# Linear attention and a two-expert layer on one core: channel-major operand stacks made by DMA transposes instead of TensorE transposes and ScalarE copies

## Chip, core and metric

The kernel runs on one core of one Trainium2 chip. The metric is the device time of one execution in microseconds (us), median of several runs; lower is better. Engines are named as in the profile: PE (TensorE matmul), PEld (its weight load), DVE (VectorE), ACT (ScalarE), POOL (GpSimd), SP (SyncE, which here only issues DMAs).

## What is computed

The input x has 8 frames of 32 channels by 64 x 64 positions (4096 tokens). Cut to what matters:

```python
def conv(x):                      # on x normalised over its channels
    q, k, v = split(einsum('bcxy,oc->boxy', x, w_qkv) + b_qkv)     # 4 heads of 32
    q = softmax(q, over the 32 channels of a head) * scale
    k = softmax(k, over the 4096 tokens)
    context = einsum('bhdn,bhen->bhde', k, v / n)
    out = einsum('bhde,bhdn->bhen', context, q)
    return layernorm_over_channels(einsum('bcxy,oc->boxy', out, w_out) + b_out) * g_ln

x = x + conv(layernorm_over_channels(x))
t = tokens(x)                     # (8, 4096, 32)
n = layernorm(t)
probs = softmax(n @ router_w + router_b)          # 8 experts
top_p, top_i = top_k(probs, 2); top_p = top_p / sum(top_p)
t = t + sum of top_p * (n @ expert_w[top_i] + expert_b[top_i])
```

## The kernel before, in words

A frame lies in SBUF token-major: 128 partitions (tokens) by 32 tiles of 32 channels, 1024 numbers a partition. Matmuls that contract over the channels need the data channel-major. For that, each of two normalised tensors (`xhat`, called k=1, which feeds keys and queries; `xhat3`, k=3, which feeds router and experts) is split into float16 parts: ACT writes the high part twice (`high_parts`, L495 and L496), DVE writes the low part (`low_part`, L684), and the rest of the 128 columns are ones. The result, `parts[k]`, is 128 x 32 x 128 float16, 1 MB. Each of its 32 tiles of 128 x 128 is transposed into `stack[k]`, 128 x 4096 float16. In the kernel before, PE does it in four units of eight transposes each into the PSUM tile `narrow` (`make_stack`, L904 to L911, recorded on L842, the line of the helper `tr`), and ACT copies each unit to SBUF (`copy_stack`, L488 to L491).

The frames run through a software pipeline written out by hand. In iteration i of the program, every engine works on up to four frames: `nxt` (frame i+1: keys, maxima, context), `cur` (frame i: queries, attention, second normalisation), `prev` (frame i-1: router, experts, output) and `ahead` (frame i+2: load and first normalisation). An iteration has 26 steps, and tables such as `AT_QEXP` or `AT_KMAX` say at which step each unit of work stands; within a step the order is that of the code, and each engine executes its own list in order. Iterations 1 to 5 are a hardware loop (`Fori`, L302); the others are written out.

The names that matter here:
- PE: `query_logits` (eight units, steps 0 to 5; matmul `narrow<-stack,w_stack` of 512 columns and four of `narrow<-qmax_tr,maxpick`); ACT exponentiates each unit into `eq` (`query_exp`, L510) and by that frees its half of `narrow`; `attend` (eight units, steps 1 to 7, `wide<-mixz,eq`); DVE normalises each into `heads` (L703, L705).
- `router` (step 4): 32 small matmuls of all of `stack[3]`; ACT copies the logits (L536), DVE picks the two experts in 14 small steps (`route`, L754 to L777, steps 4 to 8).
- `key_logits_by_channel` (steps 7 to 10, `wide<-stack,w_stack` of 512 columns), one unit for each quarter of `stack[1]`; DVE takes the maximum of each (`kmax`, L713). The key maximum is needed before the keys' exponentials and everything behind them.
- `make_stack(3)` stands at steps 1, 1, 2, 3 and `make_stack(1)` at steps 6, 6, 7, 8.
- SP issues one load of x (512 KB) and one store of y (512 KB) in an iteration, load first, and waits for the end of each store before it goes on:

```python
def store(b):
    sp.wait_ge(y_ready, OUTU * b + OUTU)
    sp.dma_start(out_v[...], y_out[:, :]).then_inc(stored, 16)
    sp.wait_ge(stored, 16 * b + 16)
    sp.sem_inc(y_free, 1)
```

Of the kernel before, what the change touches and what calls it, by code (L numbers as in the profile page):

```python
# [44 lines left out]
XT, STACK, KEXP = 2, 4, 8  # L45
# [16 lines left out]
AT_SPLIT3 = 22  # L62

AT_STACK3 = (1, 1, 2, 3)
# [16 lines left out]
AT_STACK1 = (6, 6, 7, 8)  # L81
# [15 lines left out]
def build(nc, x, w_qkv, b_qkv, w_out, b_out, g_ln, router_w, router_b, expert_w, expert_b, out):  # L97
# [6 lines left out]
    with ctx:  # L104
# [125 lines left out]
        parts_ready = {k: sem(f"parts_ready{k}") for k in (1, 3)}  # L230
        kmax_nat_ready = sem("kmax_nat_ready")
# [10 lines left out]
        y_free = sem("y_free")  # L242
# [20 lines left out]
        class Places:  # L263
# [4 lines left out]
            def __init__(self, i, cur, prev, nxt, ahead):  # L268
                if isinstance(i, int):

                    a, b, c, d = (min(max(i + k, 0), NB) for k in (2, 1, 0, -1))
                    self.w, self.n, self.s = 8 * b + 8 * c + 8 * d, 2 * a + 14 * b + 8 * c + 4 * d, 3 * b + d
                else:
                    self.w, self.n, self.s = 24 * i, 28 * i + 14, 4 * i + 2
                w = n = s = 0
                self.qexp, self.norm, self.gate, self.kmax, self.qmax = {}, {}, {}, {}, {}
                self.xt, self.qrows, self.kexp, self.stack = {}, {}, {}, {1: {}, 3: {}}
# [4 lines left out]
                for step in STEPS:  # L282
                    for there, table, at in ((ahead, self.xt, AT_XT), (prev, self.stack[3], AT_STACK3),
                                             (cur, self.qexp, AT_QEXP), (nxt, self.stack[1], AT_STACK1),
# [10 lines left out]
        def run(engine, iteration, set_up=None):  # L295
# [6 lines left out]
            with engine.Fori(1, NB - 2) as i:  # L302
                iteration(i, True, True, True, True)
# [18 lines left out]
        def _(sp):  # L322
# [157 lines left out]
        def _(act):  # L480
# [32 lines left out]
            def copy_output(g, u):  # L513
                act.wait_ge(out_full, OUTU * g + u + 1)
                if u == 0:
                    act.wait_ge(y_free, g + 1)
                nc.scalar.copy(y_out[:, 512 * u:512 * u + 512], sums[:, :]).then_inc(y_ready, 1)

            def iteration(i, cur, prev, nxt, ahead):
                f, g, n, m, pos = i, i - 1, i + 1, i + 2, Places(i, cur, prev, nxt, ahead)  # L520
                for step in STEPS:
# [6 lines left out]
                    for u in units(prev, AT_STACK3, step):  # L528
                        copy_stack(3, pos, u)
# [18 lines left out]
                    for u in units(nxt, AT_STACK1, step):  # L548
                        copy_stack(1, pos, u)
# [287 lines left out]
        def _(pe):  # L837
# [30 lines left out]
            def query_logits_by_token(pos, u):  # L868
                pe.wait_ge(narrow_free, pos.n + pos.stack[1][u] + 1)
# [34 lines left out]
            def make_stack(k, pos, b, u):  # L904
                if u == 0:
                    pe.wait_ge(parts_ready[k], 2 * b + 2)
                wait_slot(pe, narrow_free, pos.n + pos.stack[k][u], 2)
                for t in range(8):
                    ins = tr(narrow[:, pos.stack[k][u] % 2, P // 2 * t:P // 2 * t + P // 2].bitcast(f16),
                             parts[k][:, 8 * u + t, :], ident16[:])  # L910
                ins.then_inc(narrow_full, 1)  # L911

            def key_logits_by_channel(pos, u):
                pe.wait_ge(narrow_free, pos.n + pos.stack[1][u] + 1)
# [37 lines left out]
            def router(pos):  # L952
# [88 lines left out]
```

## Time and profile before

| | |
|---|---|
| runs | 587.24 us median (587.27, 586.05, 587.24) |
| span of the profiled execution | 586.6 us, 10066 instructions |
| busy | PE 412.2 us (70%), PEld 327.8 (56%), DVE 411.6 (70%), ACT 236.5 (40%), POOL 219.2 (37%) |
| DMA queue of SP | 4216 packets, 8.59 MB, 5.0% of 16 engines |
| granted TensorE clock | 0.846 of full, mean |

The profiled execution's own time isn't listed apart from its span; the span is 0.64 us below the median of the runs. An iteration of the loop takes about 63.7 us (ACT starts the casts of `parts[3]` at 168.13, 232.22, 295.91 and 359.05 us). Times of rows are from the span's start. In a timeline row the columns are start, duration, engine, line, operation, output<-input, shapes, count, and in brackets the idle time before it with what ended it.

### The profile page before, as it was taken

What the parts mean: (1) busy time and instruction counts of PE and PEld (TensorE: products, weight loads), DVE (VectorE), ACT (ScalarE), POOL (GpSimd) and SP (SyncE); (2) the same over time, 40 slices, a digit from 0 to 9 for tenths busy, and PEclk for the clock granted to TensorE, in tenths of its full rate; (3) what the DMA queues carried; (4) which work ended last, traced back from release to release, by engine and by line L of the source; (5) the groups of instructions that cost most, each with busy time, mean ns of one, the idle gap of its engine ahead of it and who ended that gap; (6) DMA issues with size and microseconds to landing.
All of it is one profiled execution on the core that took longest, in us unless ns stands there. A gap on an engine that the chain in (4) does not pass through costs nothing.

```text
span 586.6 us, 10066 instructions
## 1 busy us (share of the span) xinstructions
PE 412.2 (70%) x3632; PEld 327.8 (56%) x3632; DVE 411.6 (70%) x803; ACT 236.5 (40%) x321; POOL 219.2 (37%) x192
## 2 busy tenths in 40 slices
PE   1148968757979497958976797949894898365371
PEld 1026746645768286827765476818682786254261
DVE  0655788599757987698759975798769863964540
ACT  1043645750467125821475046712583137103200
POOL 8200563372236342552237223634255222641100
PEclk9998979786979699877989698969988898885586
DMA  2100100000011000100010001100010001000001
GB/s 50 36 1 1 37 1 7 32 1 1 1 32 41 0 0 7 59 6 0 0 37 35 0 0 30 42 0 0 5 32 0 2 2 37 1 0 15 22 0 37
DMA packets 4238, 8.90 MB, mean 15 GB/s; under 512 B 2134, under 2 KB 2168, under 8 KB 4216
## 3 DMA queue, kind: packets, MB, share of 16 engines
q1 hardware_dynamic: 4216, 8.59, 5.0%
q8 instruction: 15, 0.25, 0.2%
q14 instruction: 7, 0.06, 0.0%
HBM read 4.40 MB, written 4.19 MB: 15 GB/s over the span
## 4 chain that ended last, share of the span: by engine, by line
PE 33%; DVE 29%; issue 17%; POOL 11%; ACT 7%; DVEq 1%; POOLq 0%; ACTq 0%; PEldq 0%
PE wide L839 9%; PE sums L842 9%; PE small L839 6%; PE narrow L839 5%; PE narrow L842 4%; DVE gated L785 3%; POOL xhat L422 3%; POOL centered L417 3%; DVE kmax L713 2%; ACT stack L490 2%; DVE vsum L653 2%; DVE nsum L643 2%; DVE nqmax L690 2%; DVE tie L755 2%; DVE zrec L703 2%
## 5 line engine op out<-in xcount | busy, mean ns | idle before, releaser
L785 DVE TENSOR_TENSOR gated<-wide,gates 128x1024 f32<-128x1024 f32 x64 | 77.5, 1221 | 40.4 <-PE wide L839 37.1
L842 PE MATMUL sums<-ident,gated 128*128 128x128 f32 x512 | 79.9, 307 | 35.2 <-DVE gated L785 32.0
L502 ACT ACTIVATE ek<-narrow,wscale 128x512 f32<-128x512 f32 x64 | 44.0, 688 | 143.9 <-PE narrow L839 132.7
L842 PEld LDWEIGHTS sums<-ident,gated 128*128 128x128 f32 x512 | 65.7, 160 | 44.0 <-DVE gated L785 40.2
L839 PE MATMUL wide<-mixz,eq 128*128 128x132 f32 x512 | 73.2, 290 | 6.0 <-DVE heads L705 5.4
L490 ACT COPY stack<-narrow 128x1024 f16<-128x1024 f16 x64 | 63.0, 1013 | 34.4 <-PE narrow L842 34.3
L839 PE MATMUL wide<-w_stack,stack 128*128 128x128 f16 (+1 forms) x512 | 68.3, 279 | 6.5 <-DVE heads L705 2.6
L839 PEld LDWEIGHTS wide<-mixz,eq 128*128 128x128 f32 x512 | 64.6, 197 | 7.3 <-DVE heads L705 4.3
L839 PE MATMUL small<-ek,xhat 128*33 128x128 f32 x512 | 67.5, 278 | 0.0
L842 PE MATMUL narrow<-ident,parts 128*128 128x128 f16 x512 | 44.6, 247 | 28.0 <-ACT eq L510 18.0
L439 POOL TENSOR_TENSOR pairs<-heads 128x512 f32<-128x512 f32 x32 | 41.5, 1296 | 56.6 <-DVE heads L705 56.6
L842 PEld LDWEIGHTS narrow<-ident,parts 128*128 128x128 f16 x512 | 38.9, 112 | 33.0 <-ACT eq L510 13.6
L839 PEld LDWEIGHTS small<-ek,xhat 128*33 128x33 f32 x512 | 52.0, 112 | 9.1 <-issue 4.7
L839 PE MATMUL wide<-stack,w_stack 128*128 128x512 f16 x64 | 24.7, 477 | 44.9 <-DVE kmax L713 34.0
L839 PEld LDWEIGHTS wide<-w_stack,stack 128*128 128x128 f16 x512 | 43.9, 109 | 22.0 <-DVE kmax L713 10.0
L422 POOL TENSOR_TENSOR xhat<-centered,rstd 128x1024 f32<-128x1024 f32 x16 | 30.6, 1912 | 61.2 <-DVE rstd L679 61.2
L703 DVE RECIPROCAL zrec<-wide 128x16 f32<-128x16 f32 x64 | 16.3, 255 | 45.4 <-PE wide L839 43.3
L417 POOL TENSOR_TENSOR centered<-x_tok,nmean 128x1024 f32<-128x1024 f32 x8 | 15.3, 1912 | 81.8 <-DVE nmean L645 81.8
L705 DVE TENSOR_TENSOR heads<-wide,zrec 128x512 f32<-128x512 f32 x64 | 44.2, 691 | 2.2
L510 ACT ACTIVATE eq<-narrow,wscale 128x512 f32<-128x512 f32 x64 | 43.0, 690 | 5.4 <-PE narrow L839 5.2
L690 DVE TENSOR_REDUCE nqmax<-wide 128x32 f32<-128x1024 f32 x32 | 39.0, 1218 | 8.0 <-PE wide L839 7.9
L713 DVE TENSOR_REDUCE kmax<-wide 128x1 f32<-128x1024 f32 x32 | 38.0, 1219 | 4.7 <-PE wide L839 4.0
(138 smaller groups left out, 651.4 us busy)
## 6 DMA issues: line engine op xcount, KB each, us to landing
x_in<-in_x_dram SPq DMA_DIRECT2D x8, 512.0 KB
out_dram<-y_out SPq DMA_DIRECT2D x8, 512.0 KB
w_rows<-in_L_ffn_expert_w_dram SPq DMA_DIRECT2D x3, 32.0 KB
w_nat<-in_L_conv_w_qkv_dram SPq DMA_DIRECT2D x1, 48.0 KB
w_rows<-in_L_ffn_router_w_dram SPq DMA_DIRECT2D x3, 1.0 KB
w_rows<-in_L_ffn_expert_b_dram SPq DMA_DIRECT2D x2, 1.0 KB
w_rows<-in_L_ffn_router_b_dram SPq DMA_DIRECT2D x2, 0.0 KB
b_nat<-in_L_conv_b_qkv_dram SPq DMA_DIRECT2D x1, 1.5 KB
```

The source lines that it names most:

```text
L417: nc.gpsimd.tensor_tensor(tiles(centered[k][:]), tiles(src), per_tile(nmean[k]), ALU.add).then_inc(center_ready[k], 1)
L422: return nc.gpsimd.tensor_tensor(dst, tiles(centered[k][:]), per_tile(rstd[k]), ALU.mult)
L439: c.inc(nc.gpsimd.tensor_tensor(pairs[:, here, :], heads[:, here, 0:2 * C], heads[:, here, 2 * C:4 * C], ALU.add))
L490: nc.scalar.copy(stack[k][:, 1024 * u:1024 * u + 1024], narrow[:, pos.stack[k][u] % 2, :].bitcast(f16)).then_inc(narrow_free, 1)
L502: nc.scalar.activation(ek[:, u % EKS, :, :].rearrange("p a b -> p (a b)"), narrow[:, pos.kexp[u] % 2, :], ACT.Exp, scale=wscale[:, 0:1]).t ...
L510: nc.scalar.activation(eq[:, u % EQS, :], narrow[:, pos.qexp[u] % 2, :], ACT.Exp, scale=wscale[:, 0:1]).then_inc(narrow_free, 1)
L690: nc.vector.tensor_reduce(nqmax[:, half, 32 * (u % 2):32 * (u % 2) + 32], wide[:, pos.qmax[u] % 2, :].rearrange("p (a d) -> p a d", d=DH), ...
L705: nc.vector.tensor_tensor(heads[:, 4 * u:4 * u + 4, :].rearrange("p t (h c) -> p t h c", h=HEADS), src[:, :, 0:P].rearrange("p t (h c) -> ...
L713: nc.vector.tensor_reduce(kmax[:, u:u + 1], wide[:, pos.kmax[u] % 2, :], AX.X, ALU.max).then_inc(wide_free, 1)
L785: nc.vector.tensor_tensor(gated[:, u % GATEDS, :, :, :].rearrange("p e t c -> p t e c"), wide[:, pos.gate[u] % 2, :].rearrange("p (t e c) ...
L839: return nc.tensor.matmul(dst, lhs, rhs, start=start, stop=stop)
L842: return nc.tensor.matmul(dst, src, idt, is_transpose=True, start=start, stop=stop)
```

## The change

`make_stack` and `copy_stack` go. In their place SP issues, for each stack, four DMA transposes of 128 x 1024 float16 (256 KB each, SBUF to SBUF), each with a semaphore of its own. Those of `stack[1]` stand at step 4 of SP's list (after the last query logits of the frame before have read the stack), those of `stack[3]` at step 22, ahead of the iteration's store. The consumers on PE wait for them: `router` for all four quarters, `key_logits_by_channel` for one quarter a unit. ACT's casts wait until the transposes of the frame before have landed. SP no longer waits for a store's end before the next load; `copy_output` on ACT waits for it instead. The hardware loop is written out in Python, so no engine has loop or register instructions. The `narrow` buffers take 20 units an iteration instead of 28.

```diff
-            with engine.Fori(1, NB - 2) as i:
+            for i in range(1, NB - 2):
                 iteration(i, True, True, True, True)
...
-                sp.wait_ge(stored, 16 * b + 16)
-                sp.sem_inc(y_free, 1)
...
-            sp.sem_inc(y_free, 1)
-            load_next(1)
-            load_next(2)
-            with sp.Fori(1, NB - 2) as i:
-                load_next(i + 2)
-                store(i - 1)
-            for b in range(NB - 3, NB):
-                store(b)
+            def load_stack(k, b):
+
+                sp.wait_ge(parts_ready[k], 2 * b + 2)
+                for u in range(STACK):
+                    sp.dma_start_transpose(
+                        stack[k][:, 1024 * u:1024 * u + 1024].rearrange("p (t q) -> p t q", q=P),
+                        parts[k][:, 8 * u:8 * u + 8, :].rearrange("p t q -> p (t q)"),
+                    ).then_inc(stack_loaded[k][u], 16)
+
+            def iteration(i, cur, prev, nxt, ahead):
+                f, g, n, m, pos = i, i - 1, i + 1, i + 2, Places(i, cur, prev, nxt, ahead)
+                for step in STEPS:
+                    if ahead and step == 0 and not (isinstance(m, int) and m == 0):
+                        load_next(m)
+                    if nxt and step == AT_LOAD1:
+                        if cur:
+                            sp.wait_ge(narrow_full, pos.n + pos.qexp[7] + 1)
+                        load_stack(1, n)
+                    if cur and step == AT_LOAD3:
+                        if prev:
+                            sp.wait_ge(wide_full, pos.w + pos.gate[GATE - 1] + 1)
+                        load_stack(3, f)
+                if prev:
+                    store(g)
...
-            def copy_stack(k, pos, u):
-                act.wait_ge(narrow_full, pos.n + pos.stack[k][u] + 1)
-                nc.scalar.copy(stack[k][:, 1024 * u:1024 * u + 1024],
-                               narrow[:, pos.stack[k][u] % 2, :].bitcast(f16)).then_inc(narrow_free, 1)
...
                 act.wait_ge(xhat_ready[k], b + 1)
+                if not (isinstance(b, int) and b == 0):
+                    for u in range(STACK):
+                        act.wait_ge(stack_loaded[k][u], 16 * b)
...
-                if u == 0:
-                    act.wait_ge(y_free, g + 1)
+                if u == 0 and not (isinstance(g, int) and g == 0):
+                    act.wait_ge(stored, 16 * g)
...
-            def key_logits_by_channel(pos, u):
-                pe.wait_ge(narrow_free, pos.n + pos.stack[1][u] + 1)
+            def key_logits_by_channel(pos, n, u):
+                pe.wait_ge(stack_loaded[1][u], 16 * n + 16)
...
-            def router(pos):
-                pe.wait_ge(narrow_free, pos.n + pos.stack[3][STACK - 1] + 1)
+            def router(pos, g):
+                for u in range(STACK):
+                    pe.wait_ge(stack_loaded[3][u], 16 * g + 16)
```

The order on PE, where an iteration begins with the query logits. Before (the first units of `make_stack(3)` stand between the query logits; `L839` is the helper of matmuls, `L842` that of transposes):

```order
L839 MATMUL narrow<-stack,w_stack 128x512 [waits narrow_free]
L839 MATMUL narrow<-qmax_tr,maxpick 128x128 x4
L906 ISA
L316 REGISTER_ALU [waits parts_ready3]
L842 MATMUL narrow<-ident,parts 128x128 [waits narrow_free]
L842 MATMUL narrow<-ident,parts 128x128 x7
L316 REGISTER_ALU
```

Behind the query logits of steps 0 and 1, PE waited for `parts[3]` (`parts_ready3`) and made two units of the stack before it went on. Now, from the last query logits ahead of the router to the last query logits behind it:

```order
L850 MATMUL narrow<-qmax_tr,maxpick 128x128 x4
L850 MATMUL small<-w_stack,stack 128x8 [waits stack_loaded3_3,stack_loaded3_2,small_free,stack_loaded3_1,stack_loaded3_0]
L850 MATMUL small<-w_stack,stack 128x8 x31
L850 MATMUL wide<-mixz,eq 128x132 [waits wide_free,narrow_free]
L850 MATMUL wide<-mixz,eq 128x132 x3
L850 MATMUL narrow<-stack,w_stack 128x512 [waits narrow_free]
```

The first thing on PE that needs `stack[3]` is now the router, which waits for all four DMAs; behind it stand the attention units 3 and later and the last query logits. Further on, the key logits wait for one DMA a unit:

```order
L850 MATMUL wide<-stack,w_stack 128x512 [waits wide_free,stack_loaded1_0]
L850 MATMUL wide<-stack,w_stack 128x512
L850 MATMUL wide<-stack,w_stack 128x512 [waits wide_free,stack_loaded1_1]
```

The order on SP, one iteration of the steady part. Before (in the loop):

```order
L324 ISA [waits mean_ready1]
L324 DMA x_in<-in_x_dram 128x1x1024
L346 ISA
L347 ISA [waits y_ready]
L347 DMA out_dram<-y_out 4x32x1024
L348 ISA
L358 REGISTER_ALU [waits stored]
```

and now:

```order
L357 DMA_TRANSPOSE stack<-parts 128x8x128 [waits parts_ready3,wide_full]
L357 DMA_TRANSPOSE stack<-parts 128x8x128 x3
L347 DMA out_dram<-y_out 4x32x1024 [waits y_ready]
L324 DMA x_in<-in_x_dram 128x1x1024 [waits mean_ready1]
L357 DMA_TRANSPOSE stack<-parts 128x8x128 [waits parts_ready1,narrow_full]
```

The store and the load now stand one behind the other, between the transposes of `stack[3]` and those of `stack[1]`; no wait for the store's end is left on SP.

## Rows read from the trace of the kernel before

**Rows 1.** The profile page: the chain that ended last, share of the span by engine

```profile
PE 33%; DVE 29%; issue 17%; POOL 11%; ACT 7%; DVEq 1%; POOLq 0%; ACTq 0%; PEldq 0%
```

**Rows 2.** The page's groups: busy us, mean ns; idle before, releaser

```profile
L490 ACT COPY stack<-narrow 128x1024 f16<-128x1024 f16 x64 | 63.0, 1013 | 34.4 <-PE narrow L842 34.3
L842 PE MATMUL narrow<-ident,parts 128*128 128x128 f16 x512 | 44.6, 247 | 28.0 <-ACT eq L510 18.0
```

**Rows 3.** Timeline of PE in a loop iteration

```profile
234.85 1.89 PE L842 MATMUL narrow<-ident,parts 128*128 128x128 f16 x16 [2.49 <-ACT eq L510]
236.99 0.61 PE L839 MATMUL narrow<-stack,w_stack 128*128 128x512 f16 x1 [0.25 <-ACT stack L490]
...
238.46 1.12 PE L839 MATMUL wide<-mixz,eq 128*128 128x132 f32 x8
239.42 0.61 PE L842 MATMUL narrow<-ident,parts 128*128 128x128 f16 x8
239.86 0.38 PE L839 MATMUL narrow<-stack,w_stack 128*128 128x512 f16 x1
...
243.13 0.38 PE L839 MATMUL narrow<-stack,w_stack 128*128 128x512 f16 x1
...
243.56 0.94 PE L839 MATMUL small<-w_stack,stack 128*128 128x8 f16 x32
...
245.57 0.39 PE L839 MATMUL narrow<-qmax_tr,maxpick 128*128 128x128 f16 x4
```

**Rows 4.** Timeline of DVE in the same iteration

```profile
233.38 1.21 DVE L684 TENSOR_TENSOR parts<-xhat,parts 128x1024 f16<-128x1024 f32 x1
...
258.35 1.22 DVE L713 TENSOR_REDUCE kmax<-wide 128x1 f32<-128x1024 f32 x1
```

**Rows 5.** Windows of half a microsecond and more: engines' busy, PEclk, DMA share, GB/s

```profile
232.50:233.00 0.50, 0.00 (x0) 0.00 (x0) 0.50 (x1) 0.50 (x1) 0.00 (x0) 1.00 0.00 0
233.00:241.50 8.50, 6.40 (x60) 5.36 (x61) 4.20 (x14) 7.02 (x10) 1.91 (x1) 0.80 0.22 62
243.60:250.60 7.00, 6.32 (x92) 5.99 (x90) 6.53 (x12) 6.09 (x8) 5.63 (x7) 1.00 0.24 75
234.80:238.20 3.40, 3.10 (x22) 2.25 (x23) 1.44 (x8) 2.64 (x4) 1.64 (x1) 0.51 0.23 51
```

**Rows 6.** Timeline of SP: the store and the load of one iteration

```profile
231.76 0.60 SPq L347 DMA_DIRECT2D out_dram<-y_out  x1
242.46 0.59 SPq L324 DMA_DIRECT2D x_in<-in_x_dram  x1
```

**Rows 7.** Timeline of SP at the start: loads of the expert and router weights

```profile
4.28 0.43 SPq L337 DMA_DIRECT2D w_rows<-in_L_ffn_expert_w_dram  x1
4.75 2.15 SPq L339 DMA_DIRECT2D w_rows<-in_L_ffn_router_w_dram  x1
...
9.14 2.31 SPq L339 DMA_DIRECT2D w_rows<-in_L_ffn_router_w_dram  x1
```

**Rows 8.** Timeline of DVE at the start and at the end

```profile
35.22 1.23 DVE L684 TENSOR_TENSOR parts<-xhat,parts 128x1024 f16<-128x1024 f32 x1 [1.18 <-ACT parts L495]
40.47 4.62 DVE L713 TENSOR_REDUCE kmax<-wide 128x1 f32<-128x1024 f32 x4 [4.03 <-PE wide L839]
...
538.82 1.23 DVE L684 TENSOR_TENSOR parts<-xhat,parts 128x1024 f16<-128x1024 f32 x1 [3.10 <-ACT parts L495]
```

**Rows 9.** Timeline of PE at the end: the last frame's router

```profile
545.29 1.02 PE L839 MATMUL small<-w_stack,stack 128*128 128x8 f16 x32 [1.10 <-ACT stack L490]
```

**Rows 10.** Timeline of ACT: both casts of `parts`, in the loop and written out

```profile
232.22 1.04 ACT L495 CAST parts<-xhat 128x1024 f16<-128x1024 f32 x1 [0.63 <-POOL xhat L422]
...
243.40 1.04 ACT L495 CAST parts<-xhat 128x1024 f16<-128x1024 f32 x1
...
423.25 1.04 ACT L495 CAST parts<-xhat 128x1024 f16<-128x1024 f32 x1 [0.63 <-POOL xhat L422]
...
434.52 1.04 ACT L495 CAST parts<-xhat 128x1024 f16<-128x1024 f32 x1
```

More of the change, by code:

```diff
@@ L44 @@
 QMAX, NORM, KMAX, GATE = 4, 8, 4, 8
-XT, STACK, KEXP = 2, 4, 8
+XT, KEXP = 2, 8
+STACK = 4
 OUTU = 2
@@ L62 @@
 AT_SPLIT3 = 22
-AT_STACK3 = (1, 1, 2, 3)
+AT_LOAD3 = 22
 AT_ROUTER = 4
@@ L80 @@
 AT_SPLIT1 = 3
-AT_STACK1 = (6, 6, 7, 8)
+AT_LOAD1 = 4
 AT_KMAX = (7, 8, 9, 10)
@@ L230, in build @@
         parts_ready = {k: sem(f"parts_ready{k}") for k in (1, 3)}
+        stack_loaded = {k: [sem(f"stack_loaded{k}_{u}") for u in range(STACK)] for k in (1, 3)}
         kmax_nat_ready = sem("kmax_nat_ready")
@@ L271, in __init__ @@
                     a, b, c, d = (min(max(i + k, 0), NB) for k in (2, 1, 0, -1))
-                    self.w, self.n, self.s = 8 * b + 8 * c + 8 * d, 2 * a + 14 * b + 8 * c + 4 * d, 3 * b + d
+                    self.w, self.n, self.s = 8 * b + 8 * c + 8 * d, 2 * a + 10 * b + 8 * c, 3 * b + d
                 else:
-                    self.w, self.n, self.s = 24 * i, 28 * i + 14, 4 * i + 2
+                    self.w, self.n, self.s = 24 * i, 20 * i + 14, 4 * i + 2
                 w = n = s = 0
                 self.qexp, self.norm, self.gate, self.kmax, self.qmax = {}, {}, {}, {}, {}
-                self.xt, self.qrows, self.kexp, self.stack = {}, {}, {}, {1: {}, 3: {}}
+                self.xt, self.qrows, self.kexp = {}, {}, {}
                 if prev:
@@ L282, in __init__ @@
                 for step in STEPS:
-                    for there, table, at in ((ahead, self.xt, AT_XT), (prev, self.stack[3], AT_STACK3),
-                                             (cur, self.qexp, AT_QEXP), (nxt, self.stack[1], AT_STACK1),
+                    for there, table, at in ((ahead, self.xt, AT_XT), (cur, self.qexp, AT_QEXP),
                                              (nxt, self.kexp, AT_KEXP), (nxt, self.qrows, AT_QROWS)):
@@ L353, in load_next @@
                 load(b)
-            sp.sem_inc(y_free, 1)
-            load_next(1)
-            load_next(2)
-            with sp.Fori(1, NB - 2) as i:
-                load_next(i + 2)
-                store(i - 1)
-            for b in range(NB - 3, NB):
-                store(b)
+            def load_stack(k, b):
[20 more added lines that the diff above has]
+                    store(g)
+            run(sp, iteration)
+            sp.wait_ge(stored, 16 * NB)
         @block.gpsimd
@@ L527, in iteration @@
                                        narrow[:, pos.xt[u] % 2, :]).then_inc(narrow_free, 1)
-                    for u in units(prev, AT_STACK3, step):
-                        copy_stack(3, pos, u)
                     for u in units(cur, AT_QEXP, step):
@@ L547, in iteration @@
                         high_parts(1, n, xhat[:, :, 0:C])
-                    for u in units(nxt, AT_STACK1, step):
-                        copy_stack(1, pos, u)
                     if cur and step == AT_SQUARE2:
@@ L902, in query_logits @@
                 ins.then_inc(narrow_full, 1)
[L904 to L911, printed above, removed]
-            def key_logits_by_channel(pos, u):
-                pe.wait_ge(narrow_free, pos.n + pos.stack[1][u] + 1)
+            def key_logits_by_channel(pos, n, u):
+                pe.wait_ge(stack_loaded[1][u], 16 * n + 16)
                 wait_slot(pe, wide_free, pos.w + pos.kmax[u], 2)
@@ L987, in iteration @@
                         to_tokens(pos, m, u)
-                    for u in units(prev, AT_STACK3, step):
-                        make_stack(3, pos, g, u)
                     for u in units(cur, AT_QEXP, step):
                         query_logits(pos, u)
-                    for u in units(nxt, AT_STACK1, step):
-                        make_stack(1, pos, n, u)
                     if prev and step == AT_ROUTER:
-                        router(pos)
+                        router(pos, g)
                     for u in units(nxt, AT_KEXP, step):
```

3 lines of the change are left out of this document (1 added, 2 removed).

## The prediction

> **What bounds the kernel now.** I read the page first: no engine is full. PE and DVE are each busy 70% of the span (the table above), and the chain that ended last is shared, PE 33%, DVE 29%, issue 17%, POOL 11% [rows 1]. So the time is one of dependences within an iteration, and what counts is where the chain passes, not how busy an engine is. The page's groups say what leaves: 63.0 us of ACT's copies and 44.6 us of PE's transposes, 64 and 512 of them [rows 2]. Then I read one iteration in the timelines of PE and DVE. At its start PE has been idle for 2.49 us, runs two units of transposes, and only 0.25 us after ACT's copy comes to the next query logits at 236.99; the router starts at 243.56, and the last query logits end at 245.57 + 0.39 = 245.96 [rows 3]. On DVE the low part of `parts[3]` ends at 233.38 + 1.21 = 234.59, and the first key maximum starts at 258.35; between them the routing steps keep DVE occupied [rows 4]. SP's timeline shows the store issued at 231.76 and the load, which waited for it, at 242.46 [rows 6].
>
> **How a DMA runs here.** The window before the store's data shows no DMA, so it takes about 1.3 us from issue at 231.76 to data at 233.0; data run for 8.5 us at a share of 0.22, and 0.96 us later (241.5 to 242.46) the waiting SP goes on. The load's data take 7.0 us at a share of 0.24 [rows 5, 6]. A share of a quarter of 16 engines at 62 to 75 GB/s: these transfers keep some four engines full and leave twelve idle. I take 1.3 us ahead of a transfer's data and 1.0 us behind it.
>
> **The change, part by part.**
>
> Writing the loop out costs and gains nothing: from one cast of ACT to the other it takes 243.40 - 232.22 = 11.18 us in the loop and 434.52 - 423.25 = 11.27 us in the written-out iteration 6 [rows 10].
>
> Taking the transposes off PE: the query logits of 236.99 can start when ACT has freed `narrow`, at about 234.8. The clock is at half there (0.51 for 3.4 us, behind the idle 2.49 us [rows 3, 5]), and that idle time stays, since it ended with ACT's `eq`. Two units of query logits (243.13 to 243.56, 0.43 us each at full clock, 1.8 us together at half) and one attention unit (238.46 to 239.42, 0.96 us, 1.9 at half) end at 238.5 instead of 239.4: 0.9 us gained [rows 3]. The other two units of eight transposes (239.42 to 239.86, 0.44 us each) add as much. PE reaches the router at 243.56 - 1.8 = **241.8**. The four stack copies that leave ACT in that stretch are hidden behind the same PE work. At steps 6 to 8 DVE is behind with routing, so taking `make_stack(1)` off PE and ACT gives nothing by itself.
>
> The DMA transposes: no row shows one, so I bound t, the time for which one 256 KB transpose holds its queue and the engines. *Low end*: at the load's rate on all 16 engines, 7.0/2 x 0.24 = 0.84 us, at the store's 8.5/2 x 0.22 = 0.94 us [rows 5]; call it 0.9. *High end*: a transpose can't move 4 KB rows whole; if it goes in pieces of 256 B, it has 1024 of them, and the only run of small pieces in the trace, three times 256 + 32 pieces issued from 4.28 to 9.14 + 2.31 = 11.45 us, took 7.2/864 = 8.3 ns a piece [rows 7], hence 8.5 us. The ends are a factor of nine apart. *Taken*: t = **2.15 us**, for which the DMA behind one of 256 small pieces was held at 4.75 (2.31 at 9.14) [rows 7]. I choose by that row because a transpose, like that load and unlike the 512 KB ones, must break its rows into pieces, though I can't tell how small; it is also near the geometric middle of the ends (2.8).
>
> `stack[3]` then is complete at 234.59 + 1.3 + 4 x 2.15 + 1.0 = 245.5. PE waits 3.7 us at the router, 1.9 us later than before. Queued behind it are attention units 3 and later, the last query logits and DVE's routing. After that idle time I put PE at half clock again, and the 2.40 us from router to last query logits become some 3.9: 249.4 instead of 245.96.
>
> `stack[1]` can't be issued before 249.4, and it is behind the store and the load on SP's queue. SP is held by the four transposes until 234.6 + 8.6 = 243.2; store data from 244.5 to 253.0, load data (no wait between them now) to 260.0 on the same four engines. A transpose uses all 16, so its first quarter ends at 260.0 + 0.9 + 1.0 = 261.9, the key logits and DVE follow 0.6 us later at 262.5: **4.2 us** later than 258.35. The other quarters arrive about as fast as DVE takes them (four maxima take 4.62 us [rows 8]).
>
> The sum: iterations 1 to 5 have store and load, 5 x 4.2 = 21.0 us. Start: `parts[1]` is ready at 36.45, the last quarter at 36.45 + 1.3 + 8.6 + 1.0 = 47.35, the last maximum 1.6 us later at 48.95 instead of 45.09 [rows 8]: 3.9 us, and as much in iteration 0. Iteration 6 has no load and iteration 7 no new keys; there only the router's lateness counts, 1.9 to 3.4 us, 2.5 each. End: nothing runs beside the last frame's stack; 538.82 + 1.23 + 10.9 = 550.95 instead of 545.29 [rows 8, 9]: 5.7 us. Together 21.0 + 7.8 + 5.0 + 5.7 = 39.5 us. Against the profiled execution's span of 586.6 that is 626.1, and 0.64 us more against the median of the runs: **627 us**.
>
> **The rivals.**
>
> *Fast transposes* (t = 0.9, the low end). `stack[3]` is there at 234.59 + 1.3 + 3.6 + 1.0 = 240.5, before PE's 241.8, so 1.8 us are kept. Store data run from 239.5 to 248.0, load data to 255.0, the first maximum starts at 255.0 + 0.9 + 1.0 + 0.6 = 257.5: 0.9 us earlier. 5 x 0.9 + 2 x 1.8, 0.8 at the start, less 0.7 at the end (546.0): -8 us, **579**. If store and load don't hold the transposes back, the 1.8 us stay in every iteration: -13 us, **574**. For: the engines are three quarters idle. Against: that needs long pieces and a short issue. It decides below t = 1.14, where 253.8 + 4t passes 258.35; the router begins to wait at 1.23. The Trainium skill ("DMA: Bandwidth & Descriptors", section on latency and other measured facts) gives 261 GB/s for a DMA transpose, an estimate of 1.0 us for 256 KB, by which the sum would be about 581; no row here shows one.
>
> *In between* (t from 1.2 to 1.6): nothing to 12 us more, 587 to **600**; gain and loss cancel in part.
>
> *Piece by piece* (t = 8.5, the high end): router at 234.6 + 2.3 + 34 = 271, 27 us late, key maxima some 49 us late; five such iterations, start and end make about 410 us, **1000**. Against: it is the far end. The Trainium skill ("VectorE: DVE Perf Modes", section on the three transpose paths) gives 1309 ns for a 128 x 128 block by DMA against 390 ns on PE; if eight blocks of one instruction followed one another, an estimate of 10.5 us, the time would be above that. This trace's PE needs 0.44/8 = 0.06 us a block in a unit of eight, at full clock.
>
> *The work removed was off the chain and the stacks arrive in time anyway* (t near 1.15): no change, 587.
>
> **How the numbers follow.** Chances: t from 1.6 to 2.9 (600 to 665, my forecast) 0.45; fast, 0.28; in between, 0.13, of which 0.04 within 0.2%; above 2.9, 0.14, half of it piece by piece. At t = 2.9 the first maximum is 7.1 us late in each of five iterations, start 2 x 6.9, iterations 6 and 7 some 5 each and the end 8.7: 68 us, 655; if the four engines need all of t for their share, 10 us more. So the range is 574 to 680. A measurement can tell 0.2% (1.2 us) from no change: faster 0.29, same 0.05, slower 0.66.
>
> **What would show it.** The transposes' rows on SP: starts 2.15 us apart; 0.9 apart is the rival. PE's router waiting for a DMA 3 to 4 us in each iteration, starting about 11 us behind DVE's low part. The key logits waiting for a DMA, DVE idle 3 to 5 us ahead of the first maximum, and the period of an iteration at 68 us instead of 63.7. Store and load data running back to back at a share near 0.25, and the first transposes of `stack[1]` landing only behind them; if these land 4.5 us after their issue, the queue doesn't hold them. ACT must lose its 63 us of copies and PE its 44.6. The forecast is wrong if the router never waits.

## The result, and the profile after

The change makes the kernel a little faster: **583.89 us** median (580.23 to 589.77, 20 runs) against 587.47 us of the kernel before beside it, a ratio of 0.9931 (95% interval 0.9915 to 0.9946). The forecast was 627 us. The profiled execution has a span of 583.0 us (586.6 before) at a mean clock of 0.838 (0.846 before). One run of each kernel stood above the others, 589.77 us for the change and 813.94 us for the kernel before; neither moves the medians.

The page after: the first two lines are queue 1 and the chain by engine, the third is the key logits' group (busy us, mean ns; idle before, releaser), the fourth the issues of the transposes with their median us to landing; last comes the key logits' group of the kernel before, for comparison.

```profile
q1 hardware_dynamic: 71800, 25.38, 27.8%
...
PE 41%; DVE 26%; DMA 14%; POOL 5%; issue 5%; SPq 5%; ACT 3%; POOLq 0%; DVEq 0%; PEldq 0%; ACTq 0%
...
L850 PE MATMUL wide<-stack,w_stack 128*128 128x512 f16 x64 | 29.9, 578 | 65.2 <-DMA stack<-parts 45.2
...
stack<-parts SPq DMA_TRANSPOSE x64, 3.4
...
L839 PE MATMUL wide<-stack,w_stack 128*128 128x512 f16 x64 | 24.7, 477 | 44.9 <-DVE kmax L713 34.0
```

ACT lost nearly what was announced: it is busy 175.4 us instead of 236.5, 61.1 of the 63.0 us. PE has lost all 512 transposes, worth 44.6 us [rows 2], but is busy only 26.3 us less, 385.9 instead of 412.2, since other rows got longer: a matmul of the key logits takes 578 ns in the mean instead of 477. What came is in the chain: a seventh of it is now waiting for DMA and a twentieth SP's own issuing, where before there was neither [rows 1]. Ahead of the key logits PE was idle before too, 44.9 us, most of it for DVE's maxima; now it is 65.2 us, 45.2 of them for the DMA. So the work did leave the chain, and waits for the DMA came in.

The tile view has the size of the new operation (ns: least, median, most):

```profile
L357 SPq DMA_TRANSPOSE stack<-parts x64: 1232/1337/8337, 34.1 to 538.7; - x64
```

SP's timeline at the start, in iteration 3, and at the end:

```profile
34.06 5.48 SPq L357 DMA_TRANSPOSE stack<-parts  x4
...
232.11 5.37 SPq L357 DMA_TRANSPOSE stack<-parts  x4
237.52 0.58 SPq L347 DMA_DIRECT2D out_dram<-y_out  x1
238.14 0.55 SPq L324 DMA_DIRECT2D x_in<-in_x_dram  x1
242.05 14.93 SPq L357 DMA_TRANSPOSE stack<-parts  x4
...
534.62 5.37 SPq L357 DMA_TRANSPOSE stack<-parts  x4
```

Four transposes of `stack[3]` take SP 5.37 us, 1.34 each. Those of `stack[1]`, issued behind the store and the load, take 14.93. The windows say what the engines do meanwhile (us, busy of PE, PEld, DVE, ACT and POOL, granted clock, DMA share, GB/s):

```profile
233.40:239.00 5.60, 5.60 (x39) 4.99 (x37) 2.43 (x8) 2.52 (x5) 2.31 (x2) 0.70 1.00 188
239.00:253.50 14.50, 6.62 (x82) 5.98 (x80) 13.41 (x24) 4.34 (x7) 11.64 (x12) 0.90 0.88 80
```

While the transposes of `stack[3]` run, the share of the sixteen engines is 1.00, at 188 GB/s. Then for 14.5 us only 80 GB/s move: the store's and the load's data, near the rate of these two transfers before [rows 5]. Before, such a rate came with a share of 0.22 to 0.24; that the share is 0.88 now I read as packets of the key transposes that stand open on the other engines (not shown: in stretches of 2 us the share is 0.24 to 0.37 up to 254, but for one of 4.76, which no sixteen engines can have, so the view seems to count a packet whole where it begins). Here the GB/s are to be looked at and not the share.

PE's timeline of the iteration that [rows 3] showed before:

```profile
232.29 0.39 PE L850 MATMUL narrow<-stack,w_stack 128*128 128x512 f16 x1 [2.56 <-ACT eq L525]
...
234.89 0.63 PE L850 MATMUL narrow<-stack,w_stack 128*128 128x512 f16 x1
...
239.63 0.94 PE L850 MATMUL small<-w_stack,stack 128*128 128x8 f16 x32 [0.30 <-DMA stack<-parts]
...
241.42 0.38 PE L850 MATMUL narrow<-stack,w_stack 128*128 128x512 f16 x1
...
256.21 1.89 PE L850 MATMUL wide<-stack,w_stack 128*128 128x512 f16 x4 [8.76 <-DMA stack<-parts]
```

and DVE's, at the start, in the iteration and at the end (as [rows 4, 8]):

```profile
32.80 1.23 DVE L695 TENSOR_TENSOR parts<-xhat,parts 128x1024 f16<-128x1024 f32 x1 [1.18 <-ACT parts L510]
38.62 2.50 DVE L724 TENSOR_REDUCE kmax<-wide 128x1 f32<-128x1024 f32 x2 [4.59 <-PE wide L850]
41.31 2.37 DVE L724 TENSOR_REDUCE kmax<-wide 128x1 f32<-128x1024 f32 x2 [0.20 <-PE wide L850]
...
230.82 1.21 DVE L695 TENSOR_TENSOR parts<-xhat,parts 128x1024 f16<-128x1024 f32 x1
...
257.35 1.23 DVE L724 TENSOR_REDUCE kmax<-wide 128x1 f32<-128x1024 f32 x1 [3.29 <-PE wide L850]
...
533.33 1.23 DVE L695 TENSOR_TENSOR parts<-xhat,parts 128x1024 f16<-128x1024 f32 x1 [3.10 <-ACT parts L510]
```

The router waits 0.30 us, not 3.7. It starts 8.81 us behind DVE's low part (239.63 - 230.82); before it was 243.56 - 233.38 = 10.18. The key logits wait 8.76 us, and the first maximum comes 26.53 us behind the low part instead of 258.35 - 233.38 = 24.97: in this iteration 1.4 us won at the router and 1.6 us lost at the key maximum. That the clock falls to half behind the idle 2.56 us is as before (the granted clock is 0.50 from 234 to 236 us; the query logits of 232.29 take 0.39 us, those of 234.89, behind it, 0.63).

This iteration isn't typical. The same two distances in all five, in us from ACT's first cast of `parts[3]` to the router / to the first key maximum (e1 is the first experiment below):

| kernel | 1 | 2 | 3 | 4 | 5 | mean |
|---|---|---|---|---|---|---|
| before | 11.9 / 26.7 | 12.6 / 27.4 | 11.3 / 26.1 | 11.7 / 26.5 | 12.7 / 27.5 | 12.07 / 26.86 |
| after | 10.0 / 24.4 | 10.7 / 26.9 | 10.0 / 27.7 | 9.9 / 26.0 | 10.2 / 27.7 | 10.15 / 26.54 |
| e1_order | 10.6 / 25.1 | 10.5 / 24.9 | 10.0 / 24.4 | 10.1 / 24.6 | 10.2 / 24.7 | 10.29 / 24.75 |

Before, iteration 3 was the shortest of the five; after, it has one of the two longest ways to the maximum. **In the mean 1.9 us are won at the router, and of these 0.3 are left at the first key maximum.** In iteration 1 PE doesn't wait for a DMA at the key logits: the first store is issued only at 173.88 us, so only a load stands ahead. In iterations 2 to 5 it waits 7.30, 8.76, 7.11 and 8.55 us.

### The profile page after: what moved, and what is told of

Its sections match the earlier page's. It is cut to its first block, busy times and chain, and to the rows that moved or that the text cites. A ratio compares the mean times of both kernels' runs of the same rounds, so it can differ in the third digit from the quotient of the medians.

```text
span 583.0 us, 8031 instructions
## 1 busy us (share of the span) xinstructions
PE 385.9 (66%) x3120; PEld 299.4 (51%) x3120; DVE 412.1 (71%) x803; ACT 175.4 (30%) x257; POOL 219.2 (38%) x192
## 2 busy tenths in 40 slices
DMA packets 71838, 25.89 MB, mean 44 GB/s; under 512 B 69718, under 2 KB 69752, under 8 KB 71800
## 3 DMA queue, kind: packets, MB, share of 16 engines
q1 hardware_dynamic: 71800, 25.38, 27.8%
## 4 chain that ended last, share of the span: by engine, by line
PE 41%; DVE 26%; DMA 14%; POOL 5%; issue 5%; SPq 5%; ACT 3%; POOLq 0%; DVEq 0%; PEldq 0%; ACTq 0%
DMA stack<-parts 13%; PE sums L853 13%; PE wide L850 11%; PE small L850 11%; PE narrow L850 5%; SPq L357 5%; DVE gated L796 4%; DVE kmax L724 3%; DVE vsum L664 3%; DVE nqmax L701 2%; DVE heads L716 2%; POOL xhat L439 2%; DMA x_in<-in_x_dram 1%; DVE parts L695 1%; PE narrow L853 1%
## 5 line engine op out<-in xcount | busy, mean ns | idle before, releaser
L853 PE MATMUL sums<-ident,gated 128*128 128x128 f32 x512 | 81.4, 311 | 33.2 <-DVE gated L796 30.8
L853 PEld LDWEIGHTS sums<-ident,gated 128*128 128x128 f32 x512 | 67.0, 162 | 41.6 <-DVE gated L796 38.6
L850 PE MATMUL wide<-mixz,eq 128*128 128x132 f32 x512 | 76.7, 303 | 10.1 <-DVE heads L716 10.1
L850 PEld LDWEIGHTS wide<-mixz,eq 128*128 128x128 f32 x512 | 68.9, 209 | 11.6 <-issue 11.0
L850 PE MATMUL wide<-stack,w_stack 128*128 128x512 f16 x64 | 29.9, 578 | 65.2 <-DMA stack<-parts 45.2
L724 DVE TENSOR_REDUCE kmax<-wide 128x1 f32<-128x1024 f32 x32 | 38.2, 1220 | 15.1 <-PE wide L850 14.6
L850 PEld LDWEIGHTS wide<-stack,w_stack 128*128 128x128 f16 x64 | 4.4, 106 | 85.3 <-DMA stack<-parts 52.4
L716 DVE TENSOR_TENSOR heads<-wide,zrec 128x512 f32<-128x512 f32 x64 | 44.2, 691 | 2.2
L850 PE MATMUL narrow<-stack,w_stack 128*128 128x512 f16 x64 | 27.1, 424 | 18.6 <-ACT eq L525 18.6
L480 POOL TENSOR_TENSOR scaled<-gained,rstd 128x1024 f32<-128x1024 f32 x8 | 15.3, 1912 | 64.1 <-DVE rstd L690 64.1
```

The costliest lines, as they stand in the source:

```text
L716: nc.vector.tensor_tensor(heads[:, 4 * u:4 * u + 4, :].rearrange("p t (h c) -> p t h c", h=HEADS), src[:, :, 0:P].rearrange("p t (h c) -> ...
L724: nc.vector.tensor_reduce(kmax[:, u:u + 1], wide[:, pos.kmax[u] % 2, :], AX.X, ALU.max).then_inc(wide_free, 1)
L850: return nc.tensor.matmul(dst, lhs, rhs, start=start, stop=stop)
L853: return nc.tensor.matmul(dst, src, idt, is_transpose=True, start=start, stop=stop)
```

## Experiments

All are run beside the kernel before, in several sets, and ratios are to it (its median was 586.81 to 588.17 us). To read them, one table, worked out from ACT's first cast of `parts[3]` of each frame (for the kernel after 103.83 and 421.57; before, the latter is 423.25 [rows 10]). Its columns in us: up to the cast of iteration 1, the mean of the five iterations that follow, iteration 6, iteration 7, and what is left to the end of the span.

| kernel | start | iterations 1 to 5 | 6 | 7 | end | span |
|---|---|---|---|---|---|---|
| before | 104.7 | 63.7 | 61.3 | 53.2 | 48.9 | 586.6 |
| after | 103.8 | 63.5 | 60.1 | 50.5 | 50.8 | 583.0 |
| e1_order | 104.6 | 61.6 | 60.2 | 50.5 | 50.8 | 574.2 |
| e2_split | 103.0 | 61.5 | 60.3 | 50.5 | 44.2 | 565.4 |
| e4_unroll | 104.6 | 63.3 | 61.4 | 53.1 | 48.9 | 584.7 |
| e5_unroll_split | 103.1 | 63.2 | 62.2 | 52.6 | 42.1 | 576.0 |
| e11_only3_split | 102.3 | 61.2 | 60.1 | 51.0 | 43.8 | 563.4 |
| e12_only1_split | 102.8 | 63.1 | 62.7 | 52.0 | 42.1 | 575.2 |

**e1: the store and the load behind the transposes of `stack[1]`.** All DMAs are the same, only SP's order differs:

```diff
-                    if ahead and step == 0 and not (isinstance(m, int) and m == 0):
-                        load_next(m)
                     if nxt and step == AT_LOAD1:
...
                         load_stack(1, n)
+                    if g > 0 and step == AT_LOAD1:
+                        store(g - 1)
+                    if ahead and step == AT_LOAD1 and m != 0:
+                        load_next(m)
...
-                if prev:
-                    store(g)
 
             run(sp, iteration)
+            store(NB - 1)
```

> The changed kernel, but SP issues the store and the next load behind the four transposes of stack[1] instead of ahead of them. Theory Q (the store and load, 14.5 us of data on four engines, stand ahead of these transposes in SP's queue and make the 8.8 us idle time of PE ahead of the first key logits): the first quarter lands about 4.5 us after its issue, PE and DVE no longer wait there, 3.3 to 4 us less in each of the five steady iterations, about 572 us (568 to 577). Rival S (the transposes of stack[1] are slow by themselves): no change, 584.

Measured: 576.56 us, ratio 0.9801 (0.9775 to 0.9826), 7.3 us below the change. In PE's and DVE's timelines of its iteration 3 (cast at 228.48) no row waits for a DMA any more, save the router:

```profile
238.45 0.94 PE L851 MATMUL small<-w_stack,stack 128*128 128x8 f16 x32 [0.30 <-DMA stack<-parts]
...
246.91 0.59 PE L851 MATMUL wide<-stack,w_stack 128*128 128x512 f16 x2 [0.65 <-DVE heads L717]
...
252.92 1.22 DVE L725 TENSOR_REDUCE kmax<-wide 128x1 f32<-128x1024 f32 x1
```

The first maximum stands 24.44 us behind the cast, instead of 257.35 - 229.66 = 27.69; DVE has no idle time ahead of it, its routing steps now come last. The iterations shorten by 1.9 us in the mean, less than the 3.3 to 4 expected for each: iteration 1, where no store stood ahead, by nothing (61.4 us after, 62.2 here), iterations 2 to 5 by 1.0 to 3.7. That the key transposes stand behind store and load costs this, and is shown.

**e2: order kept, each store and load as four DMAs of 32 partitions.** It was to take away the 14.5 us without touching the order:

```diff
-                sp.dma_start(x_in[:, :], x_v[...]).then_inc(x_loaded, 16)
+                for j in range(J):
+                    sp.dma_start(x_in[C * j:C * j + C, :], x_v[b, j]).then_inc(x_loaded, 16)
```

(the store alike).

> The changed kernel with its order, but each load and store issued as four DMAs of 32 partitions, so that each should run on 16 engines instead of four. Theory Q: store and load data end about 4 us after they begin instead of 14.5 us, before the transposes of stack[1] are issued: the wait goes as in e1_order, about 573 us; the DMA share during them near 1 instead of 0.25. Rival S: 584. Rival D (a DMA's time is set by its issue or by HBM, not by its engines): data take 14 us still, 584.

Measured: 567.52 us, ratio 0.9653 (0.963 to 0.9675). SP and the windows of its iteration 3 (store from 234.75):

```profile
229.34 5.36 SPq L359 DMA_TRANSPOSE stack<-parts  x4
234.75 1.96 SPq L349 DMA_DIRECT2D out_dram<-y_out  x4
236.76 2.12 SPq L325 DMA_DIRECT2D x_in<-in_x_dram  x4
239.19 5.37 SPq L359 DMA_TRANSPOSE stack<-parts  x4
```

```profile
236.00:238.00 2.00, 1.65 (x41) 1.46 (x40) 1.95 (x3) 2.00 (x3) 1.92 (x2) 1.00 0.91 240
```

The same megabyte now moves at up to 240 GB/s on nearly all engines, and the key transposes are issued unhindered in 5.37 us instead of 14.93. The iterations are as short as in e1. The 9 us more than e1, which the expectation of 573 didn't have, are at the two ends, where the first load and the last store stand alone: 1.6 us at the start and 6.5 at the end.

**e3: both.**

> Both edits together. Theory Q: they remove the same wait, so the gains don't add: as the better of the two, 571 to 574. If each removes something of its own, under 566.

Measured: 567.16 us, ratio 0.9643 (0.9622 to 0.9665), as e2 and below the 571 to 574 expected, which left out the two ends. The two don't add: one wait, taken away in two ways.

**e4: the kernel before with its loop written out, and nothing else.**

```diff
-            with engine.Fori(1, NB - 2) as i:
+            for i in range(1, NB - 2):
```

(and SP's loop alike).

> The kernel before with only its loop written out (PE transposes and ACT copies kept). The prediction's step says it costs and gains nothing: ratio 0.998 to 1.002 to before, 586.3 to 588.5. Rival L (the register and loop instructions cost time on the chain, and the change's gain comes from their going): 581 to 585.

Measured: 583.9 us, ratio 0.9927 (0.9897 to 0.9956). The prediction's "costs and gains nothing" is refuted: this part alone gives as much as the whole change, whose ratio is 0.9931. Its profile gains 1.1 us at the very start, where PE's first transposes of x begin at 10.97 instead of 12.09,

```profile
10.97 1.94 PE L842 MATMUL narrow<-ident,x_in 128*128 128x128 f32 x8 [10.97 <-DMA x_in<-in_x_dram]
```

but that is lost again by the cast of iteration 1 (104.6 and 104.7 in the table); what stays is 1.9 us in the five iterations. The spans differ by only these 1.9 us, and the medians of this set by 3.9; the profiled run of e4 was the slowest of its six (586.47 us, the median is 583.9), so where the rest lies no profile shows. What in the loop costs the time is open too.

**e5: the control for e2**: the kernel before with the loop written out and the split of e2, still with PE's transposes.

> Control: the kernel before, loop written out, with every load and store issued as four DMAs of 32 partitions. There are no DMA transposes to hold up, so what it gains is the start (x of the first frame sooner) and the end (the last store, 6.5 us in e2_split's trace): about 584 - 9 = 575 us (573 to 578). Then e2_split's 567.5 leaves 7 to 8 us as the gain of the transposes where nothing stands ahead of them. Rival C (the four-engine transfers slow the compute engines' work, or a full load waits inside an iteration): under 572.

Measured: 576.69 us, ratio 0.9803 (0.9762 to 0.9844), as expected. So with no slow store and load beside them the DMA transposes are worth 576.7 - 567.5 = 9.2 us; in the change, 583.9 - 583.9 = 0.

This run also shows what the row was from which the prediction took t [rows 7]. SP's issue of the router's weights, first in e4, then in e5:

```profile
4.57 1.52 SPq L339 DMA_DIRECT2D w_rows<-in_L_ffn_router_w_dram  x1
...
5.55 0.45 SPq L340 DMA_DIRECT2D w_rows<-in_L_ffn_router_w_dram  x1
```

The DMA and the one ahead of it are the same; what differs is that the load of x ahead of both was one DMA in e4 and four in e5. The third issue of these weights goes from 2.20 to 0.45 us likewise. So the 2.15 us weren't the price of 256 small pieces, but most of it a hold behind the undivided load of x.

**e6: store and load, undivided, on ACT's queue**, the transposes alone on SP's. Were it SP's queue that holds the transposes, they would now be free.

> The changed kernel with its undivided store and load (four engines each) issued from ACT's queue at about the same moment as now (step 3, ahead of the casts), the transposes alone on SP's. Theory Q, as order in one queue: PE's wait for stack[1] goes, 1.1 us of issuing on ACT in its place, 575 to 579. Rival E (the four engines are busy, and whose queue it is doesn't matter): first quarter lands behind the transfers as now, 583 to 587. If the four engines alternate between the queues: in between, the last quarters late.

Measured: 599.35 us in the fastest run, the one profiled, 2.1% above the kernel before; the other three took 609.76 to 615.35 (median of all 610.38, ratio 1.0409, 1.0349 to 1.0469), and nothing is concluded from them. Even the fastest is above both expectations. PE's and DVE's rows of iteration 3 (cast at 234.30) and PE's of the last frame, a window, and the issues of ACT's and SP's queues at the last frame:

```profile
260.30 1.92 PE L851 MATMUL wide<-stack,w_stack 128*128 128x512 f16 x4 [8.18 <-DMA stack<-parts]
...
261.44 1.23 DVE L725 TENSOR_REDUCE kmax<-wide 128x1 f32<-128x1024 f32 x1 [2.70 <-PE wide L851]
...
556.58 1.00 PE L851 MATMUL small<-w_stack,stack 128*128 128x8 f16 x32 [16.26 <-DMA stack<-parts]
```

```profile
244.00:259.50 15.50, 6.38 (x77) 5.89 (x77) 13.71 (x24) 5.73 (x8) 11.41 (x12) 0.86 0.95 86
```

```profile
541.33 0.55 ACTq L491 DMA_DIRECT2D out_dram<-y_out  x1
...
543.70 10.71 SPq L349 DMA_TRANSPOSE stack<-parts  x4
```

Store and load were issued at 242.62 and 243.24, the key transposes behind them at 246.65. The key logits wait 8.18 us, as in the change (8.76), although no store or load is in SP's queue. The last frame's router waits 16.26 us, where the change has 11.83: here the store before it was issued at 541.33 from ACT, just ahead of the four transposes, and SP took 10.71 us for these instead of 5.37. No queue is shared in either place, so a transpose is held by a slow transfer whichever queue that comes from. That it is the DMA engines, which both use, is the likely reason and argued: no run parts them from anything else that the two queues may share. Of the 14.6 us by which this span is above the change's (597.6 and 583.0), 4.6 arise before the cast of iteration 1 and 5.5 behind the last; why the start is slower, and why the runs lie 16 us apart, stays open.

**e7: each transpose twice**, first into a spare tile, then as needed.

> The changed kernel with each DMA transpose issued twice, the first into a spare tile (so t, 1.34 us in the trace after, acts as 2.7). By the prediction's own sum: router 4.9 us later, store and load start 5.4 us later, first key maximum about 6 us later than before; about 50 us over the changed kernel, 634 (625 to 650). Rival H (the transposes' time is hidden by what else the queue waits for): under 600. Most time above 660: the sum misses a second wait.

Measured: 658.98 us, ratio 1.1217 (1.1165 to 1.1269), 75 us above the change and 25 above the 634 expected. SP, then PE, of its iteration 3:

```profile
259.12 1.23 SPq L361 DMA_TRANSPOSE spare<-parts  x1
260.39 1.35 SPq L365 DMA_TRANSPOSE stack<-parts  x1
...
276.32 6.42 SPq L361 DMA_TRANSPOSE spare<-parts  x1
282.78 3.37 SPq L365 DMA_TRANSPOSE stack<-parts  x1
```

```profile
272.48 0.99 PE L861 MATMUL small<-w_stack,stack 128*128 128x8 f16 x32 [6.28 <-DMA stack<-parts]
...
289.66 1.04 PE L861 MATMUL wide<-stack,w_stack 128*128 128x512 f16 x2 [8.37 <-DMA stack<-parts]
```

With t doubled to 2.7 us a quarter the router waits 6.28 us and the key logits 8.37 on top: the two waits of the forecast, both there. Iterations take 71.9 us in the mean, 8.2 more than before. The prediction's formula has the first maximum 253.8 + 4 x 2.7 - 258.35 = 6.3 us late. What it lacks is in its last step: it gives the first key quarter 0.9 us, the low end, whatever t is; with 2.7 there too it says 8.1. A kernel whose t really is 2.7 lands here at 659.

**e8: e3 with eight transposes of 128 KB for each stack; e9 with two of 512 KB; e10 with one of 1 MB.** Of e9:

```diff
-                for u in range(STACK):
+                for u in range(2):
...
-                        stack[k][:, 1024 * u:1024 * u + 1024].rearrange("p (t q) -> p t q", q=P),
-                        parts[k][:, 8 * u:8 * u + 8, :].rearrange("p t q -> p (t q)"),
+                        stack[k][:, 2048 * u:2048 * u + 2048].rearrange("p (t q) -> p t q", q=P),
+                        parts[k][:, 16 * u:16 * u + 16, :].rearrange("p t q -> p (t q)"),
```

> e3_order_split with eight transposes of 128 KB a stack instead of four of 256 KB. If a transpose's time is data (t halves to 0.67): the first quarter still needs two, last part sooner by nothing, 567 as e3 (565 to 569). If it is mostly fixed (1.2 us each whatever the size): 9.6 instead of 5.4 us a stack, router and key logits wait, 590 to 600.

> e3_order_split with each stack brought by two transposes of 512 KB instead of four of 256 KB. SP was busy 1.34 us with one of 256 KB and 1.27 us with one of 128 KB (e8). Theory F (a part of about 1.2 us fixed for each instruction, the rest small, data at most at the 240 to 290 GB/s seen where transposes stood behind one another): two take 512/265 = 1.9 us each, a stack is complete some 1.5 us sooner. The router waits at most 1.2 us in e3, in four iterations, so little of it counts there, about 1 us in all; start (last key quarter 1.5 us sooner, first 0.6 later) and end (router 1.5 us sooner) give 1 to 2 more: 565 us (563 to 567). Rival G (the time grows with the pieces again above 256 KB, 2.7 us each): no change for the router, first key quarter 1.3 us later: 567 to 570.

> The same with one transpose of 1 MB for each stack. F: 1 MB at 265 GB/s, 3.9 us: the router's stack as early as in e9, the first key quarter comes 1.9 us later than with two halves, which counts at the start and in iteration 0, and elsewhere only if the key logits have less than 2 us in hand: 566 to 571, 567 likeliest. G (5.4 us for the whole): first key quarter 4 us later at the start and in iteration 0, perhaps in others: 571 to 590.

Measured: e8 615.9 us, 1.0471 (1.043 to 1.0513); e3, for comparison, 567.16; **e9 562.74 us, 0.9609 (0.9539 to 0.9679)**, the fastest of all runs; e10 566.15 us, 0.9646 (0.9585 to 0.9708). The tile views, ns on SP:

```profile
L361 SPq DMA_TRANSPOSE stack<-parts x128: 1189/1270/2464, 33.1 to 578.5; - x128
```

```profile
L359 SPq DMA_TRANSPOSE stack<-parts x32: 1640/2182/4158, 33.1 to 521.5; - x32
```

```profile
L359 SPq DMA_TRANSPOSE stack<-parts x16: 4780/4845/4893, 33.1 to 527.4; - x16
```

128 KB take 1.27 us, 256 KB 1.34, 512 KB 2.18, 1 MB 4.85. From 128 to 256 KB it hardly grows, so there it is nearly all a fixed cost of the instruction; above that it grows with the data. A stack takes SP 10.4 us in eighths, 5.4 in quarters, 4.5 in halves, 4.85 whole. Of e9's iteration 3, the router's row has no wait left:

```profile
234.91 0.94 PE L853 MATMUL small<-w_stack,stack 128*128 128x8 f16 x32
```

e8 is even above the 590 to 600 expected for a fixed cost: its router waits for the DMA again, in iteration 3 for 4.78 us.

```profile
259.41 0.99 PE L855 MATMUL small<-w_stack,stack 128*128 128x8 f16 x32 [4.78 <-DMA stack<-parts]
```

e9 came out just below theory F's range, e10 at its low end, though a whole stack took 4.85 us and not the 3.9 expected. The intervals of e3, e9 and e10 overlap, so that halves are better than quarters by 4 us is likely and not shown; that eighths are worse is.

**e11 and e12: only one of the stacks by DMA**, the other by PE and ACT as before; both with the loop written out and the split of e2.

> stack[3] by DMA, stack[1] by PE and ACT as before, loop written out, store and load as four DMAs each. Its ends are e5 (neither by DMA, 576.7) and e2 (both, 567.5): 9.2 us. Theory A (the gain lies at the query logits ahead of the router, where make_stack(3) stood; make_stack(1) is hidden behind DVE's routing, save at the start, where its DMA brought the first maximum 1.9 us sooner): 570 us (568 to 572). Rival B (either stack is worth half): 572, and e12 the same.

> stack[1] by DMA, stack[3] by PE and ACT as before, otherwise as e11. Theory A: only the start and iteration 0 gain, 2 to 3 us of the 9.2: 574 us (572 to 577). Rival B: 572.

Measured: e11 565.44 us, ratio 0.9637 (0.9571 to 0.9704); e12 577.16 us, 0.9831 (0.9767 to 0.9895). Between the ends 576.7 (neither) and 567.5 (both), `stack[3]` alone gives the whole (2.1 us more than both, with intervals that overlap; expected were 568 to 572), and `stack[1]` alone nothing (expected were 2 to 3 us). The table says the same by iteration: 61.2 against 63.1 us. The hoped-for gain of `stack[1]` at the start isn't there either: e12's first maximum comes at 37.60, e5's, by PE, at 37.20.

## Why the prediction was wrong

The forecast was of the wrong sign: 627 us is 40 us slower than before, and 3.6 us faster came; most of the chance (0.66) was on slower. The time lies inside the range. That the sign came out as faster is the loop's doing: all of the 3.6 us are there without any DMA transpose (e4, 583.9 us), and the transposes' own gain and loss cancel.

- **t, the hold of a 256 KB transpose: the step that failed.** It was "taken 2.15 us", from a load of small pieces at the start [rows 7]; it is 1.34, between the low end (0.9) and that value. With 1.34 in the same formulas, `stack[3]` is complete at 234.59 + 1.3 + 5.4 + 1.0 = 242.3, half a microsecond behind PE's 241.8 (measured waits in iterations 2 to 5: 0.24 to 1.02), and the first maximum starts at 253.8 + 4 x 1.34 = 259.2, 0.8 us late. With 1.34 for the first key quarter too, instead of the 0.9 that the sum gave it (e7), it is 1.2 us late, 27.4 us behind the cast; the mean of iterations 2 to 5 is 27.1. So the formulas held to within some tenths and the price didn't. The row chosen was no measure of a transpose: e4 and e5 show that SP was held there behind the load of x, and without that the same issue takes 0.45 us. (The rows of this transpose are 2 KB, not the prediction's 4. The pieces of 256 B that its high end supposed are there: the queue carries 71800 - 4216 = 67584 packets more, 1056 a transpose, all under 512 B. But 1.34 us for 1056 is 1.3 ns a piece, not 8.3.) The Trainium skill ("DMA: Bandwidth & Descriptors", section on latency and other measured facts) was nearer, with 261 GB/s: estimates of 1.0 us for 256 KB and 4.0 for 1 MB, against 1.34 and 4.85 measured here. The far end, by the Trainium skill ("VectorE: DVE Perf Modes", section on the three transpose paths; 1309 ns for 128 x 128), is excluded as a price for each block: the eight blocks of one instruction take 1.34 us together.
- **PE reaches the router 1.8 us sooner: right.** In the mean of the five iterations it is 1.9 us (12.07 and 10.15 behind the cast), and e11 shows 61.2 us an iteration against 63.2 in e5, the whole worth of the transposes. That `make_stack(1)` is hidden, "gives nothing by itself": right, shown by e12.
- **The key transposes stand behind 15.5 us of store and load on four engines: right in place and size** (14.5 us at 80 GB/s; e1 and e2 remove it, 1.9 to 2.1 us an iteration in the mean). Wrong was "iterations 1 to 5 have store and load": in iteration 1 there is no store yet, and PE doesn't wait. The comparison with 258.35 and 243.56 took iteration 3, the shortest of the five, for all. And the queue isn't the reason, or not alone: another queue's store and load hold the transposes as well (e6).
- **"Writing the loop out costs and gains nothing": wrong.** e4 gives 0.73% (0.44 to 1.03). Two intervals between casts, 11.18 and 11.27 us [rows 10], said nothing of the other 52 us of an iteration or of the start. Without a gain of this size the change would have measured as no change.
- **Iterations 6 and 7: wrong in sign.** Forecast 2.5 us lost each; won 1.2 and 2.6 (e4 has none of it). There no load, or no key stack, stands behind the store, so the gain at the router stays (PE waits 3.3 us for the key stack in iteration 6, instead of 7 to 9).
- **Start: forecast 3.9 us late, and as much in iteration 0.** The parts were ready 2.4 us sooner, the last maximum ended at 41.31 + 2.37 = 43.68 instead of 45.09; from the low part to it that is 10.88 us against 9.87, 1.0 late. Iterations -1 and 0 together took 72.2 us between casts instead of 70.6, 1.5 late. Both are the mis-sized t.
- **End: forecast 5.7 us, measured 1.9** (50.8 against 48.9). The last router stands 8.76 us behind the last low part instead of 545.29 - 538.82 = 6.47; with t = 1.34 the formula gives 1.23 + 1.3 + 5.4 + 1.0 = 8.9, 2.4 late.
- **The rivals.** *In between* had the right t (1.2 to 1.6) and gave 587 to 600; the loop brought it to 584. *Fast* (its 0.8 us at the start are 1.1 by the prediction's own formula, 45.09 - 43.95) had the wrong t; its "if store and load don't hold the transposes back", 574, is near e1's 576.56, but 3.6 of that gain is the loop's, which it didn't have. Its 1.8 us kept in every iteration are borne out: 61.6 us in e1 against 63.3 in e4.

Where the gain went, in one sum of spans against e4 (584.7, the same kernel but for the transposes): start -0.8, five iterations +1.1, iterations 6 and 7 -3.9, end +1.9, together -1.7; by the medians nothing (583.89 and 583.9), since e4's profile is of its slowest run.

## What to carry to other kernels

Before moving work from a compute engine to DMA, look at what else those DMA engines carry between issue and use: here a transfer at a share of a quarter held back the transposes, from their own queue and from another, and cutting it along its outer dimension into four (e2) or issuing it behind (e1) was worth more than the move itself. When you take a price from a row, look what else was in flight there: the row that gave 2.15 us measured another transfer's hold. And compare means of all iterations, not one: the five differ by 1.4 us. Move only what stands on the path: one of the two stacks carried all of the gain, and the other only occupied the engines. Test each part of a change alone, the one that seems to be mere form (the loop) too.

## What was unexpected of the hardware

- A transpose DMA of 128 x 1024 float16 occupies SP for 1.34 us and one of half the size for 1.27: cutting finer buys nothing. One of 1 MB takes 4.85 us, four of 256 KB 5.37, two of 512 KB 4.50 (e9, two in a row at 519.78).
- 512 KB between memory and 128 partitions in one DMA moved at 62 to 75 GB/s at a share of a quarter of the engines; as four DMAs of 32 partitions the pair reached 240 GB/s. That alone, without any change to the computation, is 583.9 - 576.7 = 7.2 us (e4, e5), most of it in the last store: the end shortens from 48.9 to 42.1 us.
- Two queues don't separate two transfers: beside an undivided store of another queue, four transposes took 10.71 us instead of 5.37.
- A hardware loop of five iterations against the same code written out costs 0.73% (e4).
